# Expert result in five products of 128 rows in place of six of 96; block loops written out; y copied by ScalarE

## What is computed

```python
x = x + xattn(layernorm(x), ctx, pos, ...)
h = layernorm(x)
scores = h @ Wg.T                       # 8 experts
topk_s, topk_i = top_k(scores, 2); w = softmax(topk_s)
for e in range(8):                      # H = 176 hidden units
    a = silu(h @ W1[e].T) * (h @ W2[e].T)
    y = y + w[..., e] * (a @ W3[e].T)   # W3[e]: 256 x 176
x = x + y
```

## Time and profile before

| | |
|---|---|
| Median of 3 runs | 584.05 us (581.95 to 585.17) |
| Profiled execution | 584.55 us, span 582.8 us |
| Busy share of the span | PE 85%, PEld 65%, DVE 74%, ACT 51%, POOL 61% |
| Expert stage, PE | 377 to 540 us, 71 blocks |
| Between the attention and the expert stage | 345 to 377 us, PE clock low |
| Read-back and combination | 544 to 583 us |

### The profile page before, as it was taken

One profiled execution on the slowest core, in us unless ns is written; L12 is line 12 of the kernel. 1 busy time (PEld: TensorE's weight loads), 2 busy tenths in 40 slices (PEclk: granted clock), 3 DMA queues, 4 the chain that ended last, 5 costly groups with the idle time before them and its releaser, 6 DMA issues.

```text
span 582.8 us, 22371 instructions
## 1 busy us (share of the span) xinstructions
PE 494.8 (85%) x7781; PEld 381.6 (65%) x7782; DVE 433.6 (74%) x1245; ACT 298.0 (51%) x778; POOL 354.2 (61%) x564
## 2 busy tenths in 40 slices
PE   3889999999999999999999773799999999999000
PEld 2556666666666767666666542499999999998000
DVE  6458989898989899898989469355566655656486
ACT  3266676767676776767676443443334333343000
POOL 4756788888888888888886423034455544555200
PEclk9999999999999999999999777589999999999655
DMA  5010423232222212121111016223333333331598
GB/s 106 29 31 18 122 72 91 68 106 63 69 65 67 77 37 68 36 69 43 48 38 45 30 38 180 83 67 114 117 120 105 102 114 120 114 103 59 184 380 308
DMA packets 53190, 54.01 MB, mean 93 GB/s; under 512 B 10853, under 2 KB 48879, under 8 KB 53104
## 3 DMA queue, kind: packets, MB, share of 16 engines
q1 hardware_dynamic: 41696, 31.29, 19.1%
q0 software_dynamic: 6480, 16.82, 7.7%
q10 hardware_dynamic: 4928, 4.72, 2.4%
HBM read 29.31 MB, written 23.90 MB: 91 GB/s over the span
## 4 chain that ended last, share of the span: by engine, by line
PE 65%; DVE 19%; issue 6%; DMA 5%; ACT 2%; SPq 1%; POOL 1%; DVEq 0%; POOLq 0%; ACTq 0%
PE logit_banks L1341 13%; DVE negmax L671 10%; PE logit_banks L1359 8%; PE bank L1210 6%; PE logit_banks L1170 6%; PE qkv_banks L1119 5%; PE logit_banks L1178 5%; DMA mid<-result_rows 4%; DVE mid L656 4%; PE qkv_banks L1130 3%; PE qkv_banks L1110 3%; PE bank L1319 3%; PE qkv_banks L1350 2%; PE bank L1197 2%; PE bank L1203 2%
## 5 line engine op out<-in xcount | busy, mean ns | idle before, releaser
L610 POOL DMA_INDIRECT result_rows<-w12a,blk_dest x71 | 69.4, 977 | 89.0 <-DVE w12a L899 80.8
L577 POOL DMA_INDIRECT routed_rows<-xs,slots x64 | 65.9, 1030 | 19.3 <-issue 16.8
L671 DVE TENSOR_REDUCE negmax<-logit_banks 128x16 f32<-128x1024 f32 x64 | 75.1, 1215 | 1.0 <-PE logit_banks L1151 1.0
L1071 ACT ACTIVATE act_h<-logit_banks 128x176 f32<-128x176 f32 x71 | 22.5, 317 | 98.1 <-PE logit_banks L1341 98.1
L884 DVE TENSOR_TENSOR gated<-act_h,logit_banks 128x176 f32<-128x176 f32 x71 | 24.0, 338 | 65.1 <-ACT act_h L1071 65.1
L983 ACT ACTIVATE late<-logit_banks 128x1024 f32<-128x1024 f32 x64 | 62.0, 1021 | 17.0 <-PE logit_banks L1178 17.0
L584 POOL TENSOR_TENSOR mid<-rope_a,mid 128x512 f32<-128x512 f32 x32 | 41.1, 1284 | 32.2 <-DVE mid L656 32.2
L678 DVE RECIPROCAL rden<-bank 128x256 f32<-128x256 f32 x32 | 55.9, 1748 | 3.9 <-PE bank L1203 3.9
L1341 PE MATMUL logit_banks<-w_hi,x_hi 128*128 x142 | 48.4, 341 | 8.0 <-DVE x_lo L894 7.1
L1341 PE MATMUL logit_banks<-w_lo,x_hi 128*128 x142 | 46.9, 330 | 0.0
L1341 PE MATMUL logit_banks<-w_hi,x_lo 128*128 x142 | 46.8, 330 | 0.0
(11 more groups left out here) (179 smaller groups left out, 1344.3 us busy)
## 6 DMA issues: line engine op xcount, KB each, us to landing
xb<-routed_rows SPq DMA_DIRECT2D x71, 128.5 KB, 2.1
mid<-result_rows SPq DMA_DIRECT2D x32, 256.0 KB, 5.3
x_sb<-in_x_dram SPq DMA_DIRECT2D x32, 128.0 KB, 2.1
out_dram<-late ACTq DMA_DIRECT2D x16, 256.0 KB, 5.1
ctx_sb<-in_ctx_dram SPq DMA_DIRECT2D x32, 64.0 KB, 2.1
mid<-mT SPq DMA_DIRECT2D x128, 4.0 KB
w12a<-in_L_ffn_W_dram SPq DMA_DIRECT2D x2, 1024.0 KB, 5.8
routed_rows<-pad_row SPq DMA_DIRECT2D x11, 128.5 KB, 3.8
```

Source lines behind the costliest of these rows:

```text
L577: nc.gpsimd.indirect_dma_start(routed[:, :], bass.IndirectOffsetOnAxis(ap=slots[:, t.slot(TR), k:k + 1], axis=0), xs[:, t.slot(TR), k, :], ...
L610: nc.gpsimd.indirect_dma_start(results[:, :], bass.IndirectOffsetOnAxis(ap=blk_dest[:, b.slot(RB):b.slot(RB) + 1], axis=0), y_sb[:, b.slot ...
L671: V.tensor_reduce(negmax[:, t.par, 16 * half:16 * half + 16], ps_s[:, 1024 * half:1024 * half + 1024].rearrange("p (h k) -> p h k", k=N), ...
```

## The change

- The second chunk of hidden units holds the 48 that remain behind the first 128, padded to 64 and written twice (columns 128 to 191 and 192 to 255 of `gated`). Its weights hold the high part in rows 0 to 63 and the low part in rows 64 to 127, so that one product gives high x high and high x low. `result` has five products of 128 rows and 256 columns: high x main high, high x main low, high x rest, low x main high, low x rest. (The last adds low x low for these 48 units, which the six did not have.)
- For this W3 is loaded with its last 48 columns a second time, by two more DMAs on SP; `w3_raw` is 256 columns wide and DVE zeroes its padding and `gated` at the start (three memsets); DVE's split of a W3 bank is two subtractions (rows 0 to 127, then rows 64 to 127); `gate` is two multiplications. POOL's memsets of L618 and PE's wait for them go.
- `ended` and `ended_n` of the tables lie in the space of `w3_raw`, so DVE waits before the tables until PE has transposed banks 0 to 23.
- `blocks` writes out all turns on all engines; the expert registers are loaded at the same eight places.
- `copy_y(b-2)` moves from DVE to ACT, at the end of its turn.

```diff
-    HA = 96
-    HB = H - HA
-    OVER = HA - HB
+    H2 = 64
+    HP = P + H2
@@ buffers
-        w3_raw = sb("w3_raw", [P, KC, E, H])
-        w3_hi = sb("w3_hi", [HA, E, 2, D], FR)
+        w3_raw = sb("w3_raw", [P, KC, E, HP + H2])
+        w3_hi = sb("w3_hi", [P, E, 2, D], FR)
-        gated = sb("gated", [P, 2, H])
+        gated = sb("gated", [P, 2, HP + H2])
-        w3_lo = sb("w3_lo", [HA, E, 2, D], FR)
+        w3_lo = sb("w3_lo", [P, E, D], FR)
@@ weight_copy: what DVE subtracts, as a list
+                rest = w3_hi[H2:P, e, 1, :]
+                return (w3_hi[:, e].rearrange("p c d -> p (c d)"), ps[:, 0:2 * D],
+                        [(w3_lo[:, e], ps[:, 0:D], w3_hi[:, e, 0, :]), (rest, ps[H2:P, D:2 * D], rest)])
@@ blocks
-            for c in range(RB + 2):
-                body(do, Turn(0, c, RB))
-            rounds = (NBLK - 4) // RB
-            with eng.Fori(1, rounds) as i:
-                if prepare:
-                    prepare(i * RB)
-                for c in range(2, RB + 2):
-                    body(do, Turn(i, c, RB))
-            if prepare:
-                prepare(rounds * RB)
-            for c in range(rounds * RB + 2, NBLK + after):
+            for c in range(NBLK + after):
+                if prepare and c > RB and c < NBLK and (c - 2) % RB == 0:
+                    prepare(c - 2)
                 body(do, Turn(0, c, RB))
@@ SP, load_ffn
-                    sp.dma_start(w3_raw[:, k], W3[:, k * P:(k + 1) * P, :].rearrange("e p h -> p e h"))\
+                    sp.dma_start(w3_raw[:, k, :, 0:H], W3[:, k * P:(k + 1) * P, :].rearrange("e p h -> p e h"))\
                         .then_inc(wf3_in, 16)
+                    sp.dma_start(w3_raw[:, k, :, HP:HP + H - P],
+                                 W3[:, k * P:(k + 1) * P, P:H].rearrange("e p h -> p e h")).then_inc(wf3_in, 16)
@@ POOL
-            pool.wait_ge(wt_sb, E * KC + E)
-            for w3 in (w3_hi, w3_lo):
-                nc.gpsimd.memset(w3[0:OVER, :, 1, :].bitcast(F32), 0.0).then_inc(w3_zero, 1)
@@ DVE
             V.memset(seen[:], 0.0).then_inc(dve_const, 1)
+            V.memset(w3_raw[:, :, :, H:HP], 0.0)
+            V.memset(w3_raw[:, :, :, HP + H - P:], 0.0).then_inc(dve_const, 1)
+            V.memset(gated[:], 0.0).then_inc(dve_const, 1)
...
             dve.wait_ge(cnt_done, 1)
+            dve.wait_ge(wt_done, E * KC + E)
...
-                V.tensor_tensor(gated[:, b.par, :], act_h[:, b.par, :], ps_h[b.par][:, H:2 * H], ALU.mult)\
-                    .then_inc(gated_done, 1)
+                V.tensor_tensor(gated[:, b.par, 0:H], act_h[:, b.par, :], ps_h[b.par][:, H:2 * H], ALU.mult)
+                V.tensor_tensor(gated[:, b.par, HP:HP + H - P], act_h[:, b.par, P:H], ps_h[b.par][:, H + P:2 * H],
+                                ALU.mult).then_inc(gated_done, 1)
@@ ACT (the same function with tensor_copy goes on DVE)
+            def copy_y(b):
+                act.wait_ge(y_done, b.n + 1)
+                wait_past(act, y_out[b.slot(RB)], b.round(RB) * 16)
+                S.activation(y_sb[:, b.slot(RB), :], ps_y[b.par][:, 0:D], ACT.Copy).then_inc(y_copied, 1)
@@ PE, result
-                parts = [(h, w, c) for c in range(2) for h, w in ((h_hi, w3_hi), (h_hi, w3_lo), (h_lo, w3_hi))]
+                main, rest = w3_hi[:, bass.ds(e, 1), 0, :], w3_hi[:, bass.ds(e, 1), 1, :]
+                parts = [(h_hi, 0, main), (h_hi, 0, w3_lo[:, bass.ds(e, 1), :]), (h_hi, 1, rest),
+                         (h_lo, 0, main), (h_lo, 1, rest)]
```

More of the change, by code:

```diff
@@ L328, in weight_copy @@
             if kind == 3:
-                return (w3_hi[:, e].rearrange("p c d -> p (c d)"), w3_lo[:, e].rearrange("p c d -> p (c d)"),
-                        ps[0:HA, 0:2 * D])
+                rest = w3_hi[H2:P, e, 1, :]
+                return (w3_hi[:, e].rearrange("p c d -> p (c d)"), ps[:, 0:2 * D],
+                        [(w3_lo[:, e], ps[:, 0:D], w3_hi[:, e, 0, :]), (rest, ps[H2:P, D:2 * D], rest)])
             first = 0 if kind == 1 else H
-            return w12_hi[:, e, c, first:first + H], w12_lo[:, e, c, first:first + H], ps[:, 0:H]
+            hi = w12_hi[:, e, c, first:first + H]
+            return hi, ps[:, 0:H], [(w12_lo[:, e, c, first:first + H], ps[:, 0:H], hi)]
         def is_first(t, ahead):
@@ L815, in split_weights @@
                     dve.wait_ge(wt_hi, n + 1)
-                    hi, lo, ps = weight_copy(n)
-                    V.tensor_tensor(lo, ps, hi.bitcast(F32), ALU.subtract).then_inc(wt_sb, 1)
+                    for lo, ps, hi in weight_copy(n)[2]:
+                        ins = V.tensor_tensor(lo, ps, hi.bitcast(F32), ALU.subtract)
+                    ins.then_inc(wt_sb, 1)
             def body(do, t):
@@ L894, in split_xbT @@
                 V.tensor_tensor(x_lo[:, b.par, :], ps_tr[:, 0:D], x_hi[:, b.par, :].bitcast(F32), ALU.subtract).then_inc(bT_sb, 1)
[L896 to L899, removed]
             def ffn_body(do, b):
@@ L904, in ffn_body @@
                 do(split_xbT, b.plus(2))
-                do(copy_y, b.plus(-2))
             last_weights(split_weights, split_xbT)
@@ L914, in _ @@
             V.tensor_tensor(wtop[:, 1, :], wexp[:], wtop[:, 0, :], ALU.mult).then_inc(wtop_done, 1)
-            blocks(dve, ffn_body, 2)
+            blocks(dve, ffn_body, 1)
             def combine(i, u):
@@ L1064, in copy_hT @@
                 wait_past(act, y_done, b.n - 1)
-                S.activation(h_hi[:, b.par].rearrange("p c t -> p (c t)"), ps_hT[b.par][0:HA, 0:2 * P], ACT.Copy)\
+                S.activation(h_hi[:, b.par].rearrange("p c t -> p (c t)"), ps_hT[b.par][:, 0:2 * P], ACT.Copy)\
                     .then_inc(hT_hi, 1)
+            def copy_y(b):
+                act.wait_ge(y_done, b.n + 1)
+                wait_past(act, y_out[b.slot(RB)], b.round(RB) * 16)
+                S.activation(y_sb[:, b.slot(RB), :], ps_y[b.par][:, 0:D], ACT.Copy).then_inc(y_copied, 1)
             def silu(b):
@@ L1076, in ffn_body @@
                 do(copy_xbT, b.plus(2))
+                do(copy_y, b.plus(-2))
             last_weights(copy_weights, copy_xbT)
@@ L1080, in _ @@
             S.activation(wexp[:], wdiff[:], ACT.Exp).then_inc(wexp_done, 1)
-            blocks(act, ffn_body, 1)
+            blocks(act, ffn_body, 2)
             with act.Fori(0, T // 8) as i:
@@ L1234, in transpose_weights @@
                     if n == E * KC:
-                        pe.wait_ge(wf3_in, 32)
+                        pe.wait_ge(wf3_in, 64)
                     if n == E * KC + E:
@@ L1241, in transpose_weights @@
                     if kind == 3:
[L1242 to L1245, removed]
+                        for d in range(KC):
+                            M.transpose(ps[:, d * P:(d + 1) * P], w3_raw[:, d, e, 0:P], ident[:])
+                            ins = M.transpose(ps[:, D + d * P:D + (d + 1) * P], w3_raw[:, d, e, P:HP + H2], ident[:])
                     else:
@@ L1348, in transpose_hidden @@
                 wait_past(pe, hT_sb, b.n - 1)
-                for c in range(2):
-                    ins = M.transpose(ps_hT[b.par][0:HA, c * P:(c + 1) * P], gated[:, b.par, c * HB:c * HB + HA], ident[:])
-                ins.then_inc(hT_done, 1)
+                M.transpose(ps_hT[b.par][:, 0:P], gated[:, b.par, 0:P], ident[:])
+                M.transpose(ps_hT[b.par][:, P:2 * P], gated[:, b.par, P:HP + H2], ident[:]).then_inc(hT_done, 1)
             def result(b):
@@ L1369, in _ @@
             pe.wait_ge(wt_sb, NWT)
-            pe.wait_ge(w3_zero, 2)
             def ffn_body(do, b):
```

29 lines of the change are left out of this document (14 added, 15 removed).

## The result

The changed kernel takes 574.4 us (median of 4, 572.55 to 575.91) against 583.0 us (581.59 to 585.17) for the kernel before (median of 4; the table above has the first three): ratio 0.985, 95% interval 0.980 to 0.989. Repeated later on two other chips the ratio was 0.993 (0.989 to 0.997) and 0.988 (0.983 to 0.993). Ratios leave out runs over 1.5% above the fastest of their kernel, which the medians and ranges contain. The forecast was 575.5 us. So terms are read inside the two traces, from one event to the next, and not from the ends.

A forecast was written before the change was run, and what follows sets the result against it. PE's stream was taken to bound the expert stage, a DVE chain the passage between stages. Products -7.9, loops -1.2, between stages -0.4 and start +0.9 gave -8.6 us: 575.5 as a median, 8 in 10 within 571.5 to 578.5.

The forecast's parts named there:

- Products: Expert stage: 69 blocks each save one result product of 0.118 us; with 0.2 more for the end, -7.9 us.
- Does anything take PE's place: Expert stage: whether ACT or DVE would hold PE up in shorter blocks; claimed nothing new waits, slack 0.45 us.
- Loops written out: Expert stage: up to 3.4 us less without loop ends, 2.4 back at eight expert loads; 1.2 us less taken.
- the lead: PE's sequencer running ahead of PE before expert loads: falls from 0.8 to 0.5 us, giving 2.4 us back.
- Between the stages: DVE's chain between attention and expert stages: `cnt_i` 1.65 us less without memsets, W3 splits 1.25 more; 0.4 less.
- Start: Three memsets in DVE's stream before the first statistics, on which POOL, PE and ACT wait: 0.9 us more.
- The sum: Whole kernel: -7.9 - 1.2 - 0.4 + 0.9 = -8.6 us against the profiled 584.55 us, so 575.9; 575.5 as a median.
- W3's extra DMAs and the wait for `wt_done`: Two more SP issues fit in 4.1 us, and DVE's wait has its banks already split: both cost nothing.
- (A): Rival: written-out code stalls on its own instruction fetch; with 14 stalls 21 us more, 596.5 us; chance 0.05.
- (B): Rival: the ring of bank 7 over ACT and DVE paces the block, 2.13 us stay; 583.5 us; chance 0.06.
- (C): Rival: DVE doesn't hold the second subtraction and expert loads lose no lead; -11.85, 572.2 us; chance 0.14.
- (D): Rival: result products with 128 rows are slower than with 96; 14 us back, 589.5 us; chance 0.03.

## Why the prediction was right, point by point

- **Products**: -7.9 forecast, -9.1 measured; the term was too small. The sixth product is worth 0.12 us, as read from the rows (result products 460.46 to 461.25 before, 453.57 to 454.24 after), but the block lost 0.13, and 68 such distances make 8.8. (The other 0.01 is in the hidden products, 0.97 us in a block where they took 0.98.) The last block's is among them (1.91 and 1.78 us): the forecast took the end as hidden and charged 0.2 for the second `gate`, whose next instruction starts after 0.12. Another 0.2 to 0.4 lie in the second and third blocks, where the granted clock was rising: it went from 0.50 to 1.00 between 382 and 383 us before and between 379 and 380 us after. Those two blocks differ by as much between traces of one kernel, so this part is chance and no gain of the products.
- **Does anything take PE's place**: no, as argued. Block 2.00 (2.01 forecast), 1.88 with four products.
- **Loops written out**: -1.2 forecast and measured in the expert stage, made of 3.1 for the loops and 1.8 back for the lead, where 3.4 and 2.4 stood. Both were a little too large: the lead fell from 0.87 to 0.65 us, where 0.8 to 0.5 stood. By time the 3.1 us didn't show, on the one chip where it was tried. What y on DVE costs was not in the sum: 1 us in one trace, in longer register loads and not in a shorter lead.
- **Between the stages**: -0.4 forecast, -0.1 measured. The unblocked `cnt_i` gave 1.62 (1.65), of which putting the memsets back took away 1.5. The splits took 1.50 more (1.25): a bank costs 0.90 us and not 0.88, 0.16 over eight of them, and `cntf` behind the last one starts when that has ended, where it overlapped it by 0.08 before.
- **Start**: +0.9 forecast. This is the term that was mis-sized: 2.8 us at PE's first transposes, about 2 at tile 0's first product with `ones_row`, and more than that by time. The memsets' own time was nearly right (0.27 + 0.27 + 0.48 = 1.02 us, 1.1 in the chain, against 0.9), and what I missed is that the later POOL step meets DVE's weight copies.
- **The sum**: with the measured terms and 2.2 for the start (37.3 less 35.1), -9.1 - 1.2 - 0.1 + 2.2 = -8.2, and -0.5 more from the shorter padding writes and the tail (0.3 and 0.2 us between the two traces, single events), the sum is -8.7 beside the medians' -8.6. The agreement proves little, as the 2.2 is a mean over kernels and chips. Between the two traces alone the 12.0 us are +0.4 up to tile 0, -1.5 in the attention stage, whose code didn't change, -0.1 and -0.3 between the stages, -10.3 in the expert stage and -0.2 behind it. That the forecast of -8.6 came so close is luck in part: about 1.2 us more won at the products, 1.3 or more lost at the start. On the other two chips the medians differ by 4.3 and 8.3 us.
- **W3's extra DMAs and the wait for `wt_done`**: nothing visible, as costed; no experiment isolated them.
- **Rivals**: (A) no new stall for issue after the change, nine places as before; but by time the version with loops was not slower, so that a small cost of the written-out code outside the expert stage isn't ruled out. (B) block 2.00, not 2.13, and PE full. (C) 0.44 to 0.46 us between the subtractions, 0.33 without the hold: the hold is there, and so is the lost lead. (D) 128 rows follow each other after 0.12 us like 96.

Open is how the 2.8 us of the start shrink to about 2 by tile 0 and yet seem to cost 3 us or more in time, why the tiles of the attention stage take 9.47 us on some chips and 9.65 on others, and where block 56 loses 1.5 us on these.

## What to carry to other kernels

Before putting "only a memset" ahead of a chain, look at what the chain's later steps will then run beside: here 1.1 us of delay became 2.8, because a GpSimd step was pushed into VectorE copies. When an engine's stream is bound by its sequencer at few places, ask what each long register operation needs, and split it so that a part fits in every turn, where the sequencer waits anyway: ten registers at once cost 8 us over the stage, one per turn nothing. A product taken out of a stream gives back less than its own time where such a load stands behind it, as the lead falls too: 1.8 us back here, of 9.1. And a term read in one stage of a trace isn't yet a gain in time: 3.1 us of the loops were plain in the expert stage and absent in the medians.

## What the runs showed of the hardware

- A load of ten registers from SBUF on PE's sequencer mostly took 1.07 to 1.09 us (the first one 1.28), of seven 1.06, of one 0.30 us (71 times, 0.295 to 0.310, the first one 0.497). With y on DVE beside the five products it took 1.08 to 1.30; why is open. The Trainium skill, "Runtime: NRT & Kernel Launch", section "Instruction fetch mechanics", gives some 200 ns for each register even in bulk, for loads that the page describes as coming from HBM. By that ten would be about 2 us, an estimate; `exp_i` lies in SBUF, and the measurement decides for this case. Ten took no longer than seven, so these rows give no price per register.
- VectorE's subtractions of 256 columns start 0.33 us apart when all start at partition 0, and 0.44 to 0.46 apart when they alternate between 0 and 64.
- Beside a GpSimd memset of 16 rows by 2048 columns (1.8 us) a VectorE cast of 1 x 8 lasts until that ends (1.66 instead of 0.16 us), and beside VectorE's copies a GpSimd step of 128 x 1 took 1.94 instead of 0.23 us.
- For PE's products 96 or 128 rows made no difference (0.11 to 0.12 us from start to start for 256 columns).
